# Flamingo block on one core: who subtracts the first key parts, and where the Sync queue loads the next stack

## The reference, cut to what matters

```python
x = x + tanh(g_xattn) * xattn(layernorm(x), ctx, ctx, gamma)   # x, ctx: (16, 128, 512); 8 heads of 16 rows
x = x + tanh(g_ffn) * ffn(layernorm(x), ...)                    # 8 experts, top 2, a shared one, a core path
# xattn, by batch: q, k, v are (128, 512) = (8 heads, 16, 512)
qk  = einsum('bhdq,bhdl->bhql', q, k) / 4
ret = einsum('bhql,bhdl->bhdq', softmax(qk), v)
```

## Time and profile before

| | |
|---|---|
| median of 3 executions | 738.28 us (737.87 to 739.23) |
| the profiled execution: its time, its span | 739.24 us, 737.4 us |
| busy over the span: PE, DVE, ACT, POOL | 684.3, 531.8, 537.6, 483.7 us |
| DVE on the maxima, before the FFN | 297.9 us in 256 instructions |

### The profile page before, as it was taken

How to read it: one execution, slowest core, us unless ns; L and a number is a source line. 1 busy time by engine, 2 the same in 40 slices (tenths; PEclk the granted TensorE clock), 3 DMA queues, 4 the chain that set the end, 5 groups by cost and what they waited for, 6 DMA issues and landing times.

```text
span 737.4 us, 20876 instructions
## 1 busy us (share of the span) xinstructions
PE 684.3 (93%) x6101; PEld 372.8 (51%) x6101; DVE 531.8 (72%) x852; ACT 537.6 (73%) x1127; POOL 483.7 (66%) x477
## 2 busy tenths in 40 slices
PE   0799999899999999999989999999999999999998
PEld 0122223223333232322354554688888888888744
DVE  4989999899999999999689667744444444444456
ACT  1389999799999899999876757587676766667411
POOL 3557698878888988895667442246666666666622
PEclk9999999999999999999999999999999999999999
DMA  5756556556666756554254653789888888887487
GB/s 164 234 178 198 177 191 197 170 201 197 190 197 203 225 177 185 205 190 156 69 159 146 228 193 121 212 171 183 122 116 125 115 132 107 107 102 96 57 252 277
DMA packets 136865, 123.98 MB, mean 168 GB/s; under 512 B 70612, under 2 KB 106196, under 8 KB 136792
## 3 DMA queue, kind: packets, MB, share of 16 engines
q1 hardware_dynamic: 121928, 106.58, 50.5%
q0 software_dynamic: 13632, 15.47, 14.4%
q10 hardware_dynamic: 1232, 0.98, 0.4%
HBM read 60.33 MB, written 51.53 MB: 152 GB/s over the span
## 4 chain that ended last, share of the span: by engine, by line
PE 66%; DVE 9%; issue 7%; DMA 5%; ACT 5%; POOL 4%; SPq 2%; ACTq 0%; DVEq 0%; POOLq 0%
PE EH L1285 26%; PE Y L1285 16%; PE pv L552 9%; PE ring L539 6%; DVE mx L696 6%; PE nat L527 4%; DMA QS<-q_scratch 3%; ACT P L623 2%; DVE statx L677 1%; PE ring L571 1%; SPq L396 1%; POOL ao L748 1%; DMA QS<-mrow 1%; PE ring L562 1%; POOL un L745 1%
## 5 line engine op out<-in xcount | busy, mean ns | idle before, releaser
L696 DVE TENSOR_REDUCE mx<-nat 128x2 f32<-128x1024 f32 x256 | 297.9, 1214 | 26.9 <-PE nat L527 25.9
L623 ACT ACTIVATE P<-ring 128x512 f32<-128x512 f32 x512 | 277.3, 605 | 20.5 <-PE ring L539 12.5
L2087 POOL DMA_INDIRECT y_sums<-ysb,to x84 | 138.4, 1648 | 96.9 <-DVE ysb L2019 83.8
L552 PE MATMUL pv<-P,VT 128*32 128x256 f32 x2048 | 158.9, 394 | 0.3
L527 PE MATMUL nat<-KS,QS 48*128 48x512 f16 x512 | 109.5, 397 | 30.8 <-DMA QS<-q_scratch 22.8
L539 PE MATMUL ring<-QS,KS 49*128 49x512 f16 x512 | 120.2, 393 | 10.0 <-ACT P L623 9.2
L1633 ACT ACTIVATE X<-EH,bcur 128x256 f32<-128x256 f32 x168 | 85.6, 560 | 51.1 <-DVE u L1983 48.1
L1285 PE MATMUL Y<-whi,u 128*128 x672 | 117.1, 273 | 0.6 <-DVE u L1983 0.6
L1285 PE MATMUL EH<-XA,whi 128*128 128x256 f16 x672 | 117.0, 273 | 0.3 <-DMA XA<-g_rows 0.3
L1983 DVE TENSOR_TENSOR u<-X,u 128x512 f16<-128x512 f32 x84 | 57.7, 687 | 78.3 <-ACT u L1639 77.1
L1285 PE MATMUL Y<-wlo,u 128*128 x336 | 91.6, 273 | 0.0
(11 more groups left out here) (266 smaller groups left out, 1002.1 us busy)
## 6 DMA issues: line engine op xcount, KB each, us to landing
XA<-in_wall SPq DMA_DIRECT2D x8, 800.0 KB, 4.6
u<-in_wall SPq DMA_DIRECT2D x8, 800.0 KB, 4.5
QS<-q_scratch SPq DMA_DIRECT2D x64, 96.0 KB, 2.4
KS<-k_scratch SPq DMA_DIRECT2D x62, 96.0 KB, 2.5
X<-in_x SPq DMA_DIRECT2D x16, 256.0 KB, 2.8
q_scratch<-qhl SPq DMA_DIRECT2D x16, 256.0 KB, 2.1
xr<-in_x SPq DMA_DIRECT2D x16, 256.0 KB, 3.8
rd<-den_scratch SPq DMA_DIRECT2D x16, 256.0 KB
```

The lines of the kernel that those rows point to most:

```text
L552: m = pe.matmul(pv[32 * j:32 * j + 32, q], VT[i][:, lb, g, j, :], Pb[4 * (s % 2) + j][:, q], start=(lb == 0 and half == 0), stop=(lb == 3) ...
L623: act.activation(Pb[4 * (s % 2) + j][:, :], bank[:, :], ACT.Exp).then_inc(t_use.sem, 1)
L696: dve.tensor_reduce(mx[:, k // 8, :, k % 8], nat[k % 2][:, :, :], AX.X, ALU.max).then_inc(t_max.sem, 1)
L2087: pool.indirect_dma_start(out=ysum[:, :], out_offset=bass.IndirectOffsetOnAxis(ap=to[:, j % 2, a:a + 1], axis=0), in_=ysb[j % 2][:, a, :], ...
```

## The change

Five edits, all in the attention's program. VectorE, no longer GpSimd, subtracts batch 0's keys (`kl`), between `veps` and `qf`. GpSimd's fills of `VT` and `zs` wait for batch 0's `ql`. On SP, the first stack of keys of the next batch (`stack(ck, b, 0, 1)`) stands right behind the write of `k_scratch`, and the first stack of queries ahead of the writes of `u_rows` and `x_rows`, not behind them. The load of the third weights' part (batch 2's) stands behind the context's load. The spare zeros and the zero rows of windows 0 to 2 are issued in window 3.

```diff
-    for what in ("veps", "qf", "qh", "ql"):
+    for what in ("veps", "kl", "qf", "qh", "ql"):
         t_lead.plan(what)
...
-            jobs += [(w + 1, n) for n in (("rstd", "kl") if w < 0 else keys + queries)]
+            jobs += [(w + 1, n) for n in (("rstd",) if w < 0 else keys + queries)]
...
         def load_ctx(ck, b):
-            ck.wait(t_pool, b - 2, "kl")
+            if b == 2:
+                sp.wait_ge(t_lead.sem, t_lead.at["kl",])
+            else:
+                ck.wait(t_pool, b - 2, "kl")
...
-            if 1 <= w < B - 1:
+            if 2 <= w < B - 1:
                 load_weights(ck, w + 1)
...
             if 0 <= w < B - 2:
                 load_ctx(ck, w + 2)
+            if w == 1:
+                load_weights(ck, 2)
...
                     sp.dma_start(scr[ck.index(b), :, 2], hl[b % 2][:, high, :]).then_inc(t_.sem, 16)
+                    if side == 1:
+                        stack(ck, b, 0, 1)
...
+            if 0 <= w and b < B:
+                stack(ck, b, 0, 0)
             if s >= 0:
                 ck.wait(t_pool, s, "u")
...
-            if 0 <= w and b < B:
-                stack(ck, b, 0, 1)
-                stack(ck, b, 0, 0)
...
             if w == 0:
                 load_weights(ck, 1)
                 tail["tables"]()
+            if w == 3:
                 sp.wait_ge(t_vt.sem, 4)
                 tail["spare zeros"]()
-            if 0 <= w < B:
+                for n in range(3):
+                    tail["zeros"](ck, n)
+            if 3 <= w < B:
                 tail["zeros"](ck, w)
...
-        act.wait_ge(t_pool.sem, t_pool.at[0, "kl"])
+        act.wait_ge(t_lead.sem, t_lead.at["kl",])
         act.dma_start(sk[0, :, 0:2], khl[0][:, :, :]).then_inc(t_sk.sem, 16)
...
+            dve.wait_ge(t_lead_k.sem, t_lead_k.at["kh",])
+            dve.tensor_tensor(khl[0][:, 0, :], ct[0], khl[0][:, 1, :], ALU.subtract).then_inc(t_lead.sem, 1)
             dve.wait_ge(t_pool.sem, t_pool.at[0, "rstd"])
...
             if w < 0:
+                pool.wait_ge(t_lead.sem, t_lead.at["ql",])
                 for i in range(2):
                     pool.memset(VT[i][:, :, :, :, :], 1.0).then_inc(t_vt.sem, 1)
```

More of the change, by code:

```diff
@@ L781, in job @@
             elif what == "kl":
[L782 to L785, removed]
+                ck.wait(t_pool, b, "kh")
                 done(pool.tensor_tensor(khl[i][:, 0, :], ct[i], khl[i][:, 1, :], ALU.subtract))
```

## The result

The changed kernel takes 734.39 us in the median of 20 runs (731.28 to 738.30), the kernel before 739.17 us on the same chip (20 runs). The ratio is 0.993 with an interval of 0.9911 to 0.9949; the medians differ by 4.8 us. The profiled execution took 734.15 us, with a span of 732.3.

A forecast was written before the change was run, and what follows sets the result against it. PE, busy nearly throughout, was held by a 15.7 us head chain and by late stacks in the loop. 2.4 + 0.5 + 3.9 - 0.6 = 6.2 us gave 733.0 against the profile, 732.1 us by the median; range 729.5 to 735.6.

The forecast's parts named there:

- Head, 2.4 us: Start, up to PE's first matmul: `ql` ends earlier and the transfer follows; gain 2.4 us, 1.9 to 2.9.
- rival that `qf` is slow by itself: Head: `qf` slow without GpSimd's work, `ql` 0.6 us later than before; total gain 3.2, 735.1 us; chance 0.08.
- Window 1, 0.5 us: Window 1: PE's 0.58 us wait for `mrow` shrinks with zeros and weights moved; gain 0.5 us, 0 to 0.6.
- Loop, 3.9 us: Ten windows: the queries' stack comes some 2 us earlier, so all stalls go; gain 3.9 us, 3.0 to 4.1.
- and the half clock behind the largest with them: Loop: half clock behind the 2.10 us stall goes too; its two windows make 3.0 of the 3.9 us.
- Cost about nothing: Loop, SP: keys' read put ahead ends at 197, while reciprocals at 197.36 wait for `ql` anyway; no cost.
- PE had stood still just before: Loop, 143 to 146 us: half clock follows PE's 2.10 us stall; 16 matmuls take 1.94 instead of 1.07 us.
- Zeros, -0.6 us: Window 4: 896 KB more zeros ahead make denominators and reciprocal late; loss 0.6 us, between 0 and 4.
- loses little: Window 3: SP itself loses little to the zeros, reaching the window's end about as early; no size given.
- Slower rival: Loop: SP waits for keys' landing ahead of reciprocals; up to 4.9 us free, at 5.7 us 745.6; chance 0.05.
- FFN, nothing forecast: FFN: starts from the attention's last results and moves along; no gain or loss of its own.

The follow-up runs named there:

- head_only: Kernel before with only batch 0's `kl` on VectorE and GpSimd's fills behind `ql`: 737.31 us, ratio 0.9965.
- fills_wait: Kernel before with only GpSimd's fills waiting for batch 0's `ql`, `kl` still on GpSimd: 738.29 us in one run.
- order_only: Kernel before with only the new places of the first stacks of keys and queries on SP: 739.29 us, ratio 0.9994.
- all_three: Changed kernel with zeros in window 16, first keys' stack right ahead of the queries' stack, weights behind the context's load in every window: 741.84 us, ratio 0.9964.
- zeros_back: Changed kernel with the zeros spread over windows 0 to 3 as before: 733.12 us, ratio 0.9913.
- zeros_end: Changed kernel with the pile of zeros issued in window 16, not window 3: 732.95 us, ratio 0.9915.
- second profile: Both kernels unchanged, one more run each on the third chip: before 745.67 us, changed 738.60 us.
- weights_late: Changed kernel with the weights' load behind the context's load in every window: 766.35 us, ratio 1.0250.
- keys_late: Changed kernel with the first keys' stack right ahead of the first queries' stack: 733.10 us, ratio 0.9924.
- end_and_late: Changed kernel with zeros in window 16 and the first keys' stack right ahead of the first queries' stack: 732.62 us, ratio 0.9912.

## Why the prediction came out as it did

The forecast was 6.2 us of gain against the profiled execution; it was 5.1, and 4.8 in the medians. The direction, the range and most mechanisms held. That the sum came so near is partly luck: 0.8 of the 5.1 us is a difference in the FFN without a known cause, the zeros' cost landed in another term, and the profile that the terms were read from had the worst loop of four. By its terms:

**Head, 2.4 us: right.** `rstd` did meet the subtraction (0.95 us instead of 0.57), as taken. PE started 1.91 us earlier though the first input landed 0.58 us later in that execution (VectorE's first instruction at 4.54, before at 3.96, neither touched by the change); without that it is 2.49. `head_only` gives 2.6 us by its ratio, with an interval that takes in anything from 0.8 to 4.4. `qf` took 0.55 us, not the 0.43 of `qh`. The transfer followed: from the end of `ql` to PE's start are 5.32 us, before 5.33. The rival that `qf` is slow by itself is out, by `fills_wait`.

**Window 1, 0.5 us: right for that pair of profiles (0.60), too small for the kernel.** The wait for `mrow` of 0.58 us in the earlier trace rows is the shortest of five: the others with old zeros and old weights had 1.33, 2.16, 2.27 and 2.81, and the first to the fourth block took 33.7 to 38.4 us in these five, 35.4 in the mean. In the seven with both loads moved they took 31.9 to 34.4, in the mean 32.8. By these the term is nearer to 2.5 us, though five and seven profiles are few. The zeros' move and the weights' move each remove the wait. The ratios fit, wide as their intervals are: `head_only` has 2.6 us of the change's gain by the ratios, `order_only` none, so about half must come from these two moves; a kernel with them alone was not run. One reading of the prediction needs a correction. It calls the matmuls of the earlier trace rows at half clock, because the `pv` block at 35.75 takes 1.93 us; but the granted clock that the profile shows in 34 to 38 us is 1.00, so the rows show slow matmuls and not why. All 14 profiles have this 1.93 or 1.94 in their first block.

**Loop, 3.9 us: the step that failed as a size.** The sentence was that all stalls go, "and the half clock behind the largest with them". The stalls did go in that profile, and `order_only` had exactly the 3.9. But the changed kernel gained 1.83 of them. Window 5 lost 2.2 us again, to a wait for the denominators and the half clock behind it. The wait comes in part from the step "Cost about nothing": the prediction let the keys land 2.8 us after their write, and in windows 4 to 6 their read was issued 4.1 to 4.8 us behind it, so the reciprocals were written 12.6 and 13.3 us behind the `pv` block in windows 4 and 5, where before it was 10.5 and 10.6 (from window 7 on the keys took 1.8 us, and it did cost nothing). And the 3.9 itself was read from the worst of four executions with the old order: their ten windows took 211.73, 210.23, 208.59 and 208.37 us, so 0.6 to 3.9 above the clean 207.8. The large stall comes in some executions and not always in the same window. Over 12 runs the new order alone gives nothing that could be measured (0.9994, down to 0.9974, so at most 1.9 us). Nor is a stall enough for half clock, as the prediction's "PE had stood still just before" suggests: PE stood 2.24 us in `all_three` without it.

**Zeros, -0.6 us: right place, wrong follow-up.** The prediction had the reciprocal of window 4 less than 1 us late: it was 0.21. It is late for another reason than the one given. The transfers did not crowd: `dc` landed about 3.4 us after its issue, as elsewhere, and the spare pieces took 2.6 us, not 8.7. SP was late, which the prediction said "loses little": it issued `dc` 4.18 us behind the window's `pv` block, against 2.81 before and 1.89 in `order_only`, `zeros_back` and `zeros_end`. The prediction missed that this, with the keys' wait, could go on to window 5 (0.69) and that PE's stop there could cost clock; in the second profile it did the first and not the second. All five profiles with the pile in window 3 have the wait in window 4 (0.20, 0.21, 0.29, 1.52, 2.60), and none of the nine without it does. The pile isn't the only source: waits of 0.40, 0.81 and 0.98 came in kernels without it, in other windows. The denominators' read needs 3.5 us behind the weights, which is about when VectorE wants it, so a delay of a few tenths can show. By `weights_late` those 800 KB are 1.8 of the 3.5.

**Slower rival: a real mechanism, not reached.** SP's longest wait for the keys' landing in the changed kernel's loop was 4.4 us (by the list of waits, 22.4 us in ten of them), under the 4.9 that the prediction had as free. In `weights_late` the keys' read stood 2.7 to 7.1 us behind the end of their write's issue in the ten windows. What lies above 4.9 adds up to 11 us, and 24.6 were lost, half clock included: the mechanism was there, and its price was about twice the forecast's.

**FFN, nothing forecast: 0.8 us came.** Outside the third chip its length falls in two groups: 363.4 to 364.3 us, and 365.3 to 366.0 in `order_only`, `zeros_back`, `keys_late` and `end_and_late`. These four have a stretch at half clock between 702 and 714 us and the others have none; in `end_and_late` PE stood 1.68 us for a sum from VectorE just ahead of it. It seems to be the execution's and not the kernel's, as neither group shares an edit, and both kernels have such a stretch in their second profile, which they lacked in the first. The 0.8 us lies within the first group and has no cause that I know.

What stays open: why the first input lands 0.1 to 0.6 us later in some kernels, and what decides in which window a stall comes. A kernel clearly better than the change was not found.

## What to carry to other kernels

Before sizing a term from a stall in one profile, ask whether it is a property of the kernel or of that execution; a large stall with half clock behind it is worth its microseconds only in the executions that have it, and several smaller ones may be worth more than the one that stands out. On a shared queue an early read buys time only as long as its wait is shorter than the cover behind it, so look at what lies ahead of the data that it waits for: the same order of instructions cost nothing that could be measured or some 22 us, by the place of one 800 KB load. Keep GpSimd quiet while VectorE works on the path that starts the kernel, and that holds for fills too.

## What was unexpected of the hardware

- GpSimd's fills, which read nothing, held up VectorE's operation with one tensor input: `qf` took 3.40 us beside `kl` and the fills, 1.38 beside `kl` alone, 0.55 beside neither, and a GpSimd operation on 128x1 took 0.95 instead of 0.57 us beside a VectorE subtraction.
- A stop of PE of 0.88 us (130.00) stood ahead of a stretch at the 1.2 GHz level in one profile, while stops of 1.49 (before, 248.86) and even 2.24 us (`all_three`, 203.42) passed without it. The runs' times fall with their mean granted clock (correlation 0.9): on the straight line through them 43 runs of before, on the first two chips, come to 737.0 us at full clock and 20 of the changed kernel to 732.3. The averages lie 2.3 and 2.1 us above that: by this estimate what the stretches at half clock cost in the mean execution, against 3.0 in the two windows that the prediction read.
- The same program took 739.4 us on one chip and 745.0 on another, nearly all of the difference in the FFN (364.3 against 371.0 us in the profiles, of which stretches at half clock are a part; `all_three`, with none, has 368.7 there). The cause isn't known.
